# The three remaining expert pairs of the first token chunk written out instead of looped

## The reference

```python
def step(prev_h, xw_t):
    next_h = jnp.tanh(xw_t + prev_h @ Wh)
...
router_logits = jnp.einsum('bth,eh->bte', x, router_w)
topk_values, topk_indices = jax.lax.top_k(router_logits, TOP_K)
topk_weights = jax.nn.softmax(topk_values...)
h1 = gelu(jnp.einsum('btef...', x, w1) + b1, exact)      # 8 experts, 512 hidden units
expert_outputs = jnp.einsum('btef,ehf->bteh', h1, w2) + b2
mixed_output = sum of the two chosen experts, weighted
```

## Time and profile before

| | us |
|---|---|
| median of 3 runs | 302.99 |
| span of the profiled execution | 301.2 |
| TensorE busy, share of the span | 264.4, 88% |
| VectorE busy | 258.8, 86% |
| ScalarE busy | 215.6, 72% |
| GpSimd busy | 76.2, 25% |
| mean granted TensorE clock | 0.947 of full speed |

### The profile page before, as it was taken

How to read it: one execution, slowest core, us unless ns; L and a number is a source line. 1 busy time by engine, 2 the same in 40 slices (tenths; PEclk the granted TensorE clock), 3 DMA queues, 4 the chain that set the end, 5 groups by cost and what they waited for, 6 DMA issues and landing times.

```text
span 301.2 us, 8834 instructions
## 1 busy us (share of the span) xinstructions
PE 264.4 (88%) x2716; PEld 205.5 (68%) x2716; DVE 258.8 (86%) x635; ACT 215.6 (72%) x455; POOL 76.2 (25%) x148
## 2 busy tenths in 40 slices
PE   4969940049989999999999999999999999999994
PEld 4824440016956777778888788888777887888874
DVE  4888999989898897779988799887799988889885
ACT  6367899998842677767777676667566766689892
POOL 3367997000025413011302112212110311101000
PEclk9989976557999999999999999999999999999999
DMA  6990443101500000000000000000001000001000
GB/s 186 314 310 4 84 94 76 28 0 35 90 17 2 0 3 1 0 2 2 19 0 0 2 3 26 2 0 0 1 2 30 8 0 0 2 1 37 0 2 27
DMA packets 24031, 10.63 MB, mean 35 GB/s; under 512 B 13355, under 2 KB 22982, under 8 KB 24006
## 3 DMA queue, kind: packets, MB, share of 16 engines
q1 hardware_dynamic: 23470, 10.05, 13.6%
q10 hardware_dynamic: 536, 0.26, 0.3%
HBM read 6.11 MB, written 1.05 MB: 24 GB/s over the span
## 4 chain that ended last, share of the span: by engine, by line
PE 79%; DVE 16%; issue 1%; ACT 1%; DMA 1%; SPq 0%; DVEq 0%
PE bank L893 78%; DVE peak L706 3%; DVE big L728 3%; DVE peak L633 2%; DVE big L711 1%; DVE big L744 1%; PE bank L937 1%; DMA y_sb<-in_cond 1%; PE bank L1017 0%; DVE big L746 0%; DVE wyT L779 0%; DVE pkm L626 0%; DVE big L738 0%; DVE x_sb L759 0%; DVE q L700 0%
## 5 line engine op out<-in xcount | busy, mean ns | idle before, releaser
L893 PE MATMUL bank<-big,wt 128*128 128x384 f16 (+2 forms) x480 | 124.8, 336 | 0.6 <-DVE big L872 0.5
L893 PE MATMUL bank<-wt,big 128*128 (+1 forms) x1536 | 111.5, 219 | 0.1
L872 DVE TENSOR_TENSOR big<-big 128x384 f16<-128x384 f32 (+2 forms) x160 | 93.2, 585 | 20.5 <-ACT big L594 16.1
L893 PEld LDWEIGHTS bank<-wt,big 128*128 128x128 f16 x1536 | 97.9, 97 | 16.2 <-issue 0.2
L592 ACT ACTIVATE big<-bank,miscT 128x384 f32<-128x384 f32 (+2 forms) x160 | 96.2, 602 | 15.3 <-PE bank L893 8.2
L893 PEld LDWEIGHTS bank<-q,wxh 128*128 128x128 f32 x254 | 44.4, 189 | 17.4 <-issue 3.4
L893 PEld LDWEIGHTS bank<-big,wt 128*128 (+1 forms) x480 | 50.0, 117 | 4.8 <-issue 1.1
L580 ACT ACTIVATE q<-bank (+1 forms) x112 | 20.6, 184 | 38.7 <-PE bank L893 37.9
L404 POOL CAST big<-q 128x64 f16<-128x64 f32 x32 | 13.2, 413 | 129.0 <-ACT q L580 126.5
L868 DVE CAST big<-big 128x512 f16<-128x512 f32 (+2 forms) x104 | 38.6, 372 | 4.8 <-ACT big L592 3.9
L827 DVE SCALAR_TENSOR_TENSOR wyT<-bank,gates,wyT 128x128 f32<-128x128 f32 x128 | 39.8, 343 | 1.0 <-issue 0.6
(11 more groups left out here) (165 smaller groups left out, 320.0 us busy)
## 6 DMA issues: line engine op xcount, KB each, us to landing
wnat<-in_w SPq DMA_DIRECT2D x8, 512.0 KB, 7.7
x_sb<-in_x SPq DMA_DIRECT2D x4, 256.0 KB, 4.3
out_block<-wyT SPq DMA_DIRECT2D x15, 64.0 KB
wn<-in_w_gate ACTq DMA_DIRECT2D x1, 192.0 KB, 4.9
wn<-in_w_up SPq DMA_DIRECT2D x1, 192.0 KB, 5.6
wn<-in_w_down SPq DMA_DIRECT2D x1, 192.0 KB, 5.7
b_in<-in_b SPq DMA_DIRECT2D x12, 4.0 KB
wt<-wyT SPq DMA_TRANSPOSE x8, 3.0
```

Of the source, the lines that this page charges most:

```text
L872: V.tensor_tensor(g_lo[:, par, f, 0:w], g32[:, f, 0:w], g_hi[:, par, f, 0:w], ALU.subtract).then_inc(g_lo_done, 1)
L893: return nc.tensor.matmul(o, l, r, start=start, stop=stop, skip_group_check=True)
```

## The change

`UNROLLED = 1` is new. For chunk 0 the pairs 1 to 3 are called with integers 1, 2, 3 on all three engines, so that they stand in the program one after the other, with constant addresses and constant counts in the waits. Chunks 1 to 4 keep their loop. The extra work of the very last pair is now asked for by `is_last`, so that integer pairs of chunk 0 don't do it.

```diff
+UNROLLED = 1
...
             for c in range(CH):
                 pair(c, 0, c > 0)
-                with eng.Fori(1, E // 2 - (c == CH - 1)) as e2:
-                    pair(c, e2, True)
+                if c < UNROLLED:
+                    for e2 in range(1, E // 2):
+                        pair(c, e2, True)
+                else:
+                    with eng.Fori(1, E // 2 - (c == CH - 1)) as e2:
+                        pair(c, e2, True)
             pair(CH - 1, E // 2 - 1, True)
+
+        def is_last(c, e2):
+
+            return c == CH - 1 and isinstance(e2, int) and e2 == E // 2 - 1
...
-                    if isinstance(e2, int) and not first and s == 3:
+                    if is_last(c, e2) and s == 3:
                         take_gates(c)
...
-                    if isinstance(e2, int) and not first and s == 6:
+                    if is_last(c, e2) and s == 6:
                         add_b2(c, 2)
...
-                    if isinstance(e2, int) and not first and s == 2:
+                    if is_last(c, e2) and s == 2:
                         transpose_gates(c)
-                    if isinstance(e2, int) and not first and s == 4:
+                    if is_last(c, e2) and s == 4:
                         mix_b2(c)
```

## The result

The changed kernel takes 298.62 us (median of 4, 298.32 to 299.81) against 302.99 us (median of 4). The ratio is 0.9871, 95% interval 0.9846 to 0.9896: faster by 1.3%. The profiled execution has a span of 297.2 us, 4.0 less than before. The granted TensorE clock is 1.00 in all of these stretches, from 80 us to the last matmul, in the kernel before and in the changed one, so it has no part in the differences.

A forecast was written before the change was run, and what follows sets the result against it. The prediction took TensorE to bound the kernel, its chunk 0 loop slowed by register addresses and counts. 5.10 us saved less 0.53 us for VectorE gave 4.57 us, so 298.4 us, range 297.7 to 300.2 us.

The forecast's parts named there:

- The bound: From chunk 1's start at 130.26 us the chain is TensorE alone, so chunk 0's savings reach the end in full.
- TensorE's stream held up by register addresses: Chunk 0's looped slots take 1.15 us against 0.81 written out, because TensorE's instructions arrive late with addresses and counts from registers.
- All of it lies on the path: Chunk 0's three pairs on TensorE fall from 23.46 to 18.36 us, 5.10 us less, all of it on the path.
- VectorE late next, 0.53 us: In pair 1, slot 10's down group waits for VectorE's late low part, handing back 0.53 us once.
- ScalarE's 0.02 us of room: After a two-Gelu slot the tanh is ready at 1.80 us, wanted at 1.82; costed at nothing, bound 1.2 us.
- Start of chunk 1: Chunk 1 waits for the last tanh, done 0.55 + 0.18 us into slot 31, before that slot's end; costed at nothing.
- Chunks 1 to 4 untouched: The pace of chunks 1 to 4, which keep their loop, was held to stay as before.
- The sum: 5.10 - 0.53 = 4.57 us less: span from 301.2 to 296.6 us, median from 302.99 to 298.4 us.
- The turn-only case: Rival, 6%: only the loop's turn in chunk 0 counts, three turns gaining 0.7 to 0.9 us, 302.2 us.
- an estimate of 0.3 us: If a loop cost only its compare-and-branch, about 108 ns each, the change would be worth 0.3 us.
- The given-back case: Rival, 15%: late tanh on ScalarE and late casts on VectorE give 1.7 us back, 2.9 us gained, 300.1 us.
- The code case: Rival, 4%: written-out code fetched too late, three TensorE page crossings at 1.7 us, 0.5 us slower, 303.5 us.

The follow-up runs named there:

- k5: The kernel before with its loops, but constant weight and recurrence addresses on TensorE in chunk 0's looped pairs (wrong results): pairs 1 to 3 20.31 us, median 299.44 us.
- k1: The changed kernel, but only TensorE has chunk 0's pairs written out; ScalarE and VectorE keep their loop: pairs 20.30 us, median 300.57 us, ratio 0.9930.
- k2: The changed kernel, but only ScalarE and VectorE have chunk 0's pairs written out; TensorE keeps its loop: pairs 23.15 us, median 302.40 us, ratio 0.9996.
- k11: The changed kernel, but VectorE keeps its loop in chunk 0; TensorE and ScalarE are written out: pairs 19.22 us, 300.71 us in one run.
- k10: As k5, but constant addresses on TensorE in the looped pairs of chunk 1 too: pairs 20.30 us, chunk 1 36.93 us, 298.51 us in one run.
- k7: The changed kernel with all chunks written out, no loop left: pairs 19.22 us, chunk 1 36.93 us, median 297.74 us, ratio 0.9855.
- k6: The changed kernel with chunks 0 and 1 written out: pairs 19.22 us, chunk 1 36.92 us, median 298.13 us, ratio 0.9843.
- k8: The changed kernel with chunk 0's last five gate operations moved from VectorE to GpSimd: pairs 18.65 us, median 298.41 us, ratio 0.9869.
- k9: As k8, but with chunks 0 and 1 written out: pairs 18.64 us, chunk 1 36.93 us, median 296.95 us, ratio 0.9818.

## Why the prediction was right

**The bound.** Right. What the three pairs gave up reached the end: the distance from pair 1's start to the last matmul fell by 3.94 us (187.95 to 184.01), and the pairs by 4.19. Chunk 2 and what follows kept their lengths (47.56 us for chunk 2 in both).

**TensorE's stream held up by register addresses.** Right, and shown by k5 with the loop left in place. The prediction's argument for it was weaker than the result: it took the third wide matmul, late with nothing new to wait for, as proof. In k1 TensorE has constant addresses, and that matmul is late too (0.24 us behind the recurrence matmul, against 0.22 in the loop and 0.14 at full pace), only because the tanh was. So the rows that it showed did not rule out waits for the tanh. The trace does for their slot, where the tanh ends at 110.85 us, 0.27 us ahead of the recurrence matmul at 111.12, and k2 and k5 do for the three pairs.

**"All of it lies on the path", priced as TensorE's alone.** The 5.10 us was right as a sum, but not as TensorE's doing: 3.16 us are TensorE's, and 1.03 us came only because ScalarE was written out as well (k1, k11). The prediction took the written-out tanh latency of 0.33 us without saying that the loop's was longer. Had the change been made on TensorE alone, this step would have been 1 us too high.

**VectorE late next, 0.53 us.** Right in place and kind, the down group of slot 10; it measured 0.62. The low part came at 108.76 and not 108.70 and took 0.49 us instead of 0.42, behind a cast of 0.36 instead of 0.29. The cadence of 5.68 us a pair held well enough that no second wait for VectorE appeared.

**ScalarE's 0.02 us of room, costed at nothing.** It held in five of six places. In the sixth, slot 25, the Gelu of slot 23 started 0.35 us after its tanh instead of 0.12, 0.16 us of it idle with nothing to wait for, and the tanh behind it made TensorE lose 0.13 us. ScalarE and then TensorE in the changed kernel:

```profile
119.40 0.18 ACT L589 ACTIVATE q<-bank 128x16 f32<-128x16 f32 x1 [0.21 <-PE bank L902]
119.75 0.47 ACT L601 ACTIVATE big<-bank,miscT 128x256 f32<-128x256 f32 x1 [0.16 <-issue]
120.12 0.47 ACT L603 ACTIVATE big<-bank,miscT 128x256 f16<-128x256 f32 x1
120.47 0.18 ACT L589 ACTIVATE q<-bank 128x16 f32<-128x16 f32 x1
```

```profile
120.46 0.38 PE L902 MATMUL bank<-big,wt 128*128 128x256 f16 x2
120.71 0.40 PE L902 MATMUL bank<-q,wxh 128*128 128x16 f32 x2
120.95 0.27 PE L902 MATMUL bank<-big,wt 128*128 128x256 f16 x1
...
121.39 0.49 PE L902 MATMUL bank<-big,wt 128*128 128x256 f16 x3
```

**Start of chunk 1, costed at nothing.** Low by 0.10 us: the last tanh ends 0.73 us into slot 31, as reckoned, but the input part starts 0.90 us into it, after a hop of 0.17 us that I had left out.

**Chunks 1 to 4 untouched.** Wrong by 0.25 us: chunk 1 rose from 37.40 to 37.65, around the turns of its own loop. The first in the changed kernel took 1.41 us (144.84 to 146.25) and the second 1.42, where the kernel before has 1.34 and 1.36; the slots before and behind the second turn took 1.17 and 1.20 us instead of 1.12 and 1.13. Why the turns differ between kernels (37.36 to 37.65 over all with this loop) was not tried.

**The sum.** 4.57 us expected, 3.94 found between two points of the traces, 4.37 between the medians. The difference of the first two is 0.09 + 0.13 + 0.10 + 0.25 = 0.57, and rounding. That the median came within 0.2 us of the forecast is partly luck: inside the trace 0.63 us of the forecast gain is missing.

**The rivals.** The turn-only case falls by k5 and k10: k5 and k1 differ by 0.01 us over the three passes of the loop. Its price counted three turns; only two are there to see, the first slots of pairs 2 and 3. The figure for a compare-and-branch in the Trainium skill, page "Advanced Engine Details and Errata", section Control Flow Timing, from which the prediction made an estimate of 0.3 us, finds no counterpart in these runs. That the branches are hidden behind queued matmuls would explain it, but is only argued. The given-back case came true to about an eighth of its price (0.13 + 0.09 of 1.7 us). The code case falls by k7, where 21 packets came without a hole near the 1.7 us a page of its price. The Trainium skill, page "Runtime: NRT & Kernel Launch", section Instruction fetch mechanics, has fetching mostly hidden, and k7 agrees, but for a gap of 0.16 us on ScalarE that may belong to it (last section).

## What to carry to other kernels

Before writing out a loop, compare the starts of the same instructions inside it and in a written-out copy: where they stand further apart, the stream may be late, and a loop over narrow matmuls with register addresses is where to expect it. The rows alone don't prove it, since a late tanh makes the instructions behind it late as well; a loop with constant addresses does, at the price of one run with wrong results. Cost each engine's loop by itself, since two may be slow and hide each other, and work out beforehand which wait stands next, for it can be as cheap to remove as it is to find. Wide slots hide the same address work, so that writing out more code stops paying there.

## What was not expected

The addresses matter and the branch does not: with constant addresses on TensorE a loop ran as fast as no loop in chunk 0 (20.31 against 20.30 us) and in chunk 1 (36.93 against 36.92).

ScalarE has a late Gelu with no cause that the list of waits shows, in the same place of the program, the Gelu of slot 23, in all seven kernels in which ScalarE's chunk 0 is written out (119.75 us in the changed kernel, 119.70 in k6, 118.60 in k7, 122.03 in k2, 0.16 us each) and in none of the six in which it is looped. In each of the seven a packet of q14, the second code queue, starts about half a microsecond behind it (between 120.2 and 120.4 us in the changed kernel, between 122.6 and 122.8 in k2), and in the six there is none at that place. So the turn of a code page on ScalarE is a candidate. It is not shown: the trace doesn't say for which engine a packet is, the Gelu starts before it, and the kernel before has two gaps of 0.16 us on ScalarE in later loops, at 243.59 and 254.95 us, without such a packet near. No run moved it.

The part before pair 1, the same on TensorE in all kernels, ended between 105.66 and 107.16 us over the twelve profiles beside the kernel before. The granted clock there is not the same from profile to profile: in the four that ended it first (k7, k8, k10 and k9, by 106.04 us) it was 1.00 over the first 30 us, in the others 0.94. That scatter alone makes whole times of four or five runs too coarse for differences under 0.3%.
